# Decoder layer on one core: attention of the last row issued later, the first gate/up tile decoded in the first row's prologue and kept in DRAM, four products of zeros at TensorE's start

## The reference, cut to what matters

```python
x = _layernorm(x + attn(x, weight_qkv, weight_proj))           # causal, over the outer axis of length 4
x = _layernorm(x + ssm(ctx_1024, x, in_proj_w, conv_w, ...))   # state space scan over 512 steps, 16 states
x = _layernorm(x + ffn(x, lut, gate_idx, up_idx, down_idx))

def step(state, xs):                                           # the scan, for each of 4 rows
    d_t, B_t, C_t, u_t = xs
    dA = jnp.exp(d_t[..., None] * A)
    state = state * dA + (d_t * u_t)[..., None] * B_t[:, None, :]
    y_t = jnp.einsum('ben,bn->be', state, C_t)
    return (state, y_t)

def _ghost_linear(x, idx, lut):                                # weights are 4-bit indices into 16 values
    w = lut[idx]
    return jnp.einsum('bsh,oh->bso', x, w)
gate = _ghost_linear(x, gate_idx, lut)
up = _ghost_linear(x, up_idx, lut)
h = jax.nn.silu(gate) * up
return _ghost_linear(h, down_idx, lut)
```

## Time and profile before

| | |
|---|---|
| median of 3 runs | 990.57 us (990.4 to 994.05) |
| the profiled execution's own time | 990.59 us |
| its span in the trace | 988.8 us |
| prologue, until DVE's first scan | 0 to 55.0 us |
| scan of the four rows | 55 to 538 us |
| transition, until the first gate/up product | about 552 to 602.6 us |
| feed-forward | 602.6 to 988.8 us |
| busy share of the span | PE 88%, DVE 77%, ACT 68%, POOL 49% |

### The profile page before, as it was taken

One profiled execution on the slowest core, in us unless ns is written; L12 is line 12 of the kernel. 1 busy time (PEld: TensorE's weight loads), 2 busy tenths in 40 slices (PEclk: granted clock), 3 DMA queues, 4 the chain that ended last, 5 costly groups with the idle time before them and its releaser, 6 DMA issues.

```text
span 988.8 us, 11890 instructions
## 1 busy us (share of the span) xinstructions
PE 869.3 (88%) x3824; PEld 626.4 (63%) x3824; DVE 765.2 (77%) x1066; ACT 672.4 (68%) x994; POOL 481.3 (49%) x445
## 2 busy tenths in 40 slices
PE   6879888787878897787989879899999999899997
PEld 3547654465544674456545457787777778688885
DVE  3797899877998879986788666888888888355442
ACT  4698985789956899668696464777777776242321
POOL 0079867799767998669676631221112111001000
PEclk9789777999779797787979988999999999899998
DMA  8167979589996799967999222111111110223221
GB/s 259 39 168 177 209 161 229 117 221 245 210 224 122 204 241 210 224 125 202 208 289 277 83 96 86 46 61 42 42 42 44 62 42 22 75 86 107 86 64 53
DMA packets 49908, 135.99 MB, mean 138 GB/s; under 512 B 5364, under 2 KB 13684, under 8 KB 41156
## 3 DMA queue, kind: packets, MB, share of 16 engines
q0 software_dynamic: 8064, 58.72, 30.9%
q1 hardware_dynamic: 40432, 76.44, 23.1%
q10 hardware_dynamic: 1364, 0.25, 0.2%
HBM read 57.93 MB, written 78.51 MB: 138 GB/s over the span
## 4 chain that ended last, share of the span: by engine, by line
PE 26%; issue 23%; DVE 23%; ACT 19%; POOL 5%; DMA 4%; DVEq 1%; ACTq 0%; POOLq 0%; SPq 0%
DVE state L1191 6%; PE banks L606 5%; ACT decay L893 5%; PE banks L720 5%; ACT scaled L882 5%; PE banks L744 4%; DVE leaf L1219 3%; DVE w_gu L1219 3%; PE banks L644 3%; PE banks L548 3%; DVE conv_in L1094 3%; POOL state L1442 2%; ACT leaf L1001 2%; DMA hT<-y_scratch 2%; DMA y_scratch<-state 1%
## 5 line engine op out<-in xcount | busy, mean ns | idle before, releaser
L1442 POOL TENSOR_TENSOR state<-state,crep 128x512 f32<-128x512 f32 x243 | 334.8, 1603 | 85.9 <-DVE state L1191 79.7
L1191 DVE TENSOR_TENSOR_SCAN state<-decay,banks 128x512 f32<-128x512 f32 x243 | 280.7, 1202 | 54.2 <-PE banks L644 44.6
L720 PE MATMUL banks<-x2T,wgu 128*128 128x512 f32 x1056 | 246.3, 393 | 4.8 <-DVE hT L1270 4.1
L644 PE MATMUL banks<-ident,scaled 128*128 128x128 f32 x1024 | 175.9, 314 | 69.1 <-DVE state L1191 49.7
L720 PEld LDWEIGHTS banks<-x2T,wgu 128*128 128x128 f32 x1056 | 197.9, 189 | 52.1 <-DVE hT L1270 11.3
L644 PEld LDWEIGHTS banks<-ident,scaled 128*128 128x128 f32 x1024 | 136.2, 161 | 143.1 <-DVE state L1191 63.4
L893 ACT ACTIVATE decay<-delta,negA 128x512 f32<-128x512 f32 x256 | 169.9, 722 | 77.6 <-DVE state L1191 69.8
L882 ACT ACTIVATE scaled<-duT,BT 128x512 f32<-128x512 f32 x256 | 163.8, 720 | 0.0
L1001 ACT ACTIVATE leaf<-idx_sb,table,table_gap 128x1024 f32<-128x1024 uint8 (+1 forms) x132 | 129.4, 1022 | 6.8 <-DVE w_down L1219 3.2
L1219 DVE COPY_PREDICATED leaf<-idx_sb,leaf 128x1024 f32<-128x1024 uint8 (+1 forms) x88 | 94.1, 1069 | 7.1 <-issue 6.1
L1534 POOL TENSOR_TENSOR pool_wait_here<-minus_half 128x1 f32<-128x1 f32 x22 | 4.3, 193 | 180.6 <-DVE w_gu L1219 116.2
(11 more groups left out here) (140 smaller groups left out, 1155.6 us busy)
## 6 DMA issues: line engine op xcount, KB each, us to landing
y_scratch<-state POOLq DMA_DIRECT2D x52, 1024.0 KB, 8.5
crep<-c_scratch SPq DMA_DIRECT2D x64, 256.0 KB, 5.4
idx_sb<-in_idx SPq DMA_DIRECT2D x11, 512.0 KB, 3.5
xT_sb<-in_xT SPq DMA_DIRECT2D x16, 256.0 KB, 4.8
y_scratch<-u SPq DMA_DIRECT2D x4, 1024.0 KB, 6.1
y_scratch<-state SPq DMA_DIRECT2D x4, 1024.0 KB, 6.3
leaf<-x_scratch SPq DMA_DIRECT2D x16, 256.0 KB, 2.8
out<-leaf SPq DMA_DIRECT2D x16, 256.0 KB, 2.0
```

The source lines that it names most:

```text
L644: last = nc.tensor.transpose(banks[:, k % NB, lc * LQ:(lc + 1) * LQ], scaled[:, g % SR, lc, et * P:(et + 1) * P], ident[:])
L720: last = mm(banks[:, 2 * tb + w, :], wgu[par][:, w, ws, t * P:(t + 1) * P], x2T[:, tb, xs, t, :], start=t == 0 and n == 0, stop=t == HT - ...
L1191: V.tensor_tensor_scan(state[:, g % GR, et, :], decay[:, k % DR_RING, :], banks[:, k % NB, :], 0.0, ALU.mult, ALU.add).then_inc(scan_ready, 1)
L1442: G.tensor_tensor(state[:, g % GR, et, :], state[:, g % GR, et, :], crep[:, g % CR, :], ALU.mult)\
```

## The change

Three edits in one, and what they entail.

1. LAST_ATT_AT, LAST_PROJ_AT and LAST_RES_AT: in the last row four attention jobs, two projections and two residuals stand later; ACT's copies of them, its `normalized`, and POOL's `norm_factors` move with them.
2. The gate/up tile 0 is decoded in the prologue, in space that the scan does not use yet (`state` for the leaves, `scaled` for the indices, `decay` for the table): all eight leaves on POOL, seven predicated copies on DVE, the result stored to `w0_scratch` by SP early in the first row and loaded into `w_gu` late in the last row. FIRST's decoding in the transition goes, on ACT, DVE and POOL, and the loads of SECOND and of the first `down` tile are issued where the loads of FIRST and SECOND were, two states later. POOL's second `gate_row` comes behind two of its reciprocal roots.
3. PE runs WARM = 4 products of zeros before it waits for `ip`; POOL fills the zeros.

```diff
+        WARM = 4
-        LAST_ATT_AT = {(3, 0): 3, (3, 1): 0, (4, 0): 2, (5, 0): 1}
+        LAST_ATT_AT = {(3, 3): 3, (4, 0): 0, (4, 2): 2, (6, 1): 1}
-        LAST_PROJ_AT = {(5, 1): 3, (5, 3): 2, (6, 1): 1, (6, 3): 0}
+        LAST_PROJ_AT = {(5, 1): 3, (5, 3): 2, (7, 0): 1, (7, 2): 0}
-                LAST_RES_AT = {(5, 2): 3, (6, 0): 2, (6, 2): 1, (7, 0): 0}
+                LAST_RES_AT = {(5, 2): 3, (6, 0): 2, (7, 1): 1, (7, 3): 0}
...
+        FIRST_MUX = [(0, 1, 1), (2, 3, 1), (0, 2, 2), (4, 5, 1), (6, 7, 1), (4, 6, 2), (0, 4, 3)]
...
@@ SP
                 load_xT(0)
+                sp.dma_start(first_words, idx[0, :, 0:2 * H]).then_inc(first_idx_in, 16)
                 sp.dma_start(wqkv[:], wqkvT.rearrange("(t p) n -> p t n", p=P)).then_inc(wqkv_in, 16)
...
+                        if n == 0 and b == 0:
+                            sp.wait_ge(first_mux_ready, 7)
+                            sp.dma_start(w0_scratch, first_leaf(0)).then_inc(first_stored, 16)
...
-                        if b == S - 1 and n == 11:
+                        if b == S - 1 and n == 13:
                             sp.dma_start(table[:], lut.to_broadcast([P, 16])).then_inc(lut_in, 16)
-                            load_idx(*FIRST)
+                            sp.wait_ge(first_stored, 16)
+                            sp.dma_start(w_gu[:].rearrange("p w n -> p (w n)"), w0_scratch).then_inc(first_in, 16)
                             load_idx(*SECOND)
+                            load_idx("down", 0)
...
@@ PE
+                pe.wait_ge(zeros_ready, 1)
+                for _ in range(WARM):
+                    mm(banks[:, 7, :], state[:, 0, 0, 0:P], state[:, 0, 0, :], start=True, stop=True)
                 pe.wait_ge(ip_in, 16)
...
@@ ACT
+                act.dma_start(first_table, lut.to_broadcast([P, 16])).then_inc(first_lut_in, 16)
                 act.wait_ge(ch_in, 16)
...
                 act.wait_ge(gap_ready, 1)
-                leaves(*FIRST, early)
+                high_part(0, 0)
                 norm_apply(0)
-                leaves(*FIRST, (4, 5))
                 norm_apply(1)
                 x2T_hi(0)
-                leaves(*FIRST, (6,))
...
@@ DVE
+                def first_selects(steps):
+                    for m in steps:
+                        kept, other, bit = FIRST_MUX[m]
+                        dve.wait_ge(first_leaf_ready, max(kept, other) + 1 if m < 6 and bit == 1 else 8)
+                        if m in (2, 5, 6):
+                            dve.wait_ge(first_mux_ready, m)
+                        V.memset(first_wait[:, m:m + 1], 0.0)
+                        V.copy_predicated(first_leaf(kept), first_bit(bit), first_leaf(other)).then_inc(first_mux_ready, 1)
...
+                dve.wait_ge(first_lut_in, 16)
+                first_pairs = first_table.rearrange("p (j two) -> p j two", two=2)
+                V.tensor_tensor(first_gap, first_pairs[:, :, 1], first_pairs[:, :, 0], ALU.subtract).then_inc(first_gap_step, 1)
+                dve.wait_ge(first_gap_step, 1)
+                V.tensor_scalar(first_gap, first_gap, 0.5, None, ALU.mult).then_inc(first_gap_step, 1)
                 dve.wait_ge(ch_in, 16)
                 for et in range(ET):
                     earlier_taps(0, et)
+                    if et == 1:
+                        dve.wait_ge(first_idx_in, 16)
+                        V.tensor_scalar(first_words, first_words, float(SPREAD), None, ALU.mult).then_inc(first_bits_step, 1)
+                    elif et == 2:
+                        dve.wait_ge(first_bits_step, 1)
+                        V.tensor_scalar(first_words, first_words, BYTE_BITS, None, ALU.bitwise_and)\
+                            .then_inc(first_bits_step, 1)
...
+                first_selects(range(5))
                 softplus(0, (0, 1))
                 softplus(0, (2, 3))
+                first_selects((5, 6))
                 head_products(0, 3)
...
-                MUXES = [(FIRST, (0, 1)), (FIRST, (2, 3)), (FIRST, (4, 5)), (FIRST, (6,)), (SECOND, ()),
-                         (SECOND, (0, 1)), (SECOND, (2, 3)), (SECOND, (4,))]
+                MUXES = [(), (), (), (), (), (0, 1), (2, 3), (4,)]
...
@@ POOL
+                G.memset(state[:, 0, 0, :], 0.0).then_inc(zeros_ready, 1)
                 G.memset(minus_half[:], -0.5).then_inc(half_ready, 1)
                 pool.wait_ge(half_ready, 1)
+                pool.wait_ge(first_gap_step, 2)
+                pool.wait_ge(first_bits_step, 2)
+                for j in range(8):
+                    G.tensor_tensor(first_wait[:, 8 + j:9 + j], minus_half[:, 0:1], minus_half[:, 0:1], ALU.add)
+                    G.tensor_scalar(first_leaf(j), first_bit(0), first_gap[:, j:j + 1], first_table[:, 2 * j:2 * j + 1],
+                                    ALU.mult, ALU.add).then_inc(first_leaf_ready, 1)
...
                 gate_row(1)
-                last_leaf(*FIRST)
+                stage2_rstd(0)
+                stage2_rstd(1)
                 gate_row(2)
-                for k in range(5):
+                for k in range(2, 5):
                     stage2_rstd(k)
```

65 lines of the change are left out of this document (39 added, 26 removed).

## The result

| | before | after |
|---|---|---|
| median of 5 runs | 990.57 us (990.33 to 994.05) | 1001.19 us (998.55 to 1001.91) |
| profiled execution, its span | 990.59, 988.8 us | 998.55, 996.7 us |

The changed kernel is slower by 0.88%: the ratio is 1.0088, 95% interval 1.0069 to 1.0106. Measured once more beside the later experiments it was 1.0097 (1.0076 to 1.0118). The two medians stand further apart than the ratio says: 10.6 us, 1.07%. The median lies 7.5 us above the forecast and 1.2 us above the upper end of the range; the ratio on 990.57 us gives 999.3 us, 5.6 us above the forecast and just inside.

What follows compares the result with a forecast made beforehand. The prediction took DVE's work and waits to bound the prologue, PE waits and adding transfers the last row, DVE's low parts the transition. Terms 9.0 + 0.5 - 6.4 = +3.1 us on 990.59 gave 993.7 us, range 985 to 1000.

Steps and rivals of the forecast that it cites:

- rival (c): Whole kernel slower: late table, slow kv products; prologue +12, last row +2, transition -5, 999.6 us; chance 0.27.
- Prologue, +9.0: Up to the first scan: late table, index operations, leaves and copies delay it by 9.0 us, to 64.0 us.
- the point of decision of rival (c): Prologue: a table later than 13.5 us or a leaf chain longer than 15 us would decide for rival (c).
- the zeros' gain: Prologue: products of zeros bring `in_proj`'s first bank 2.0 us earlier, but DVE's wait for the table loses it.
- Last row, +0.5: Last row: `hT` lands 1.75 us earlier, `rest_summed` costs 2.2 us more; sum +0.5 us.
- In the last row no wait of DVE on PE over 3 us: Last row, expected sign: DVE's long waits on PE go, while waits on `y_scratch<-state` grow longer.
- The 2.2 us for `rest_summed` on an idle PE: Row's end: PE's last sums finish some 9 us ahead of `hT`, so `rest_summed` starts slowly, costing 2.2 us.
- Transition, -6.4: Transition: without copies between statistics and shift, residual(4) loses its 4.31 us wait and 2.1 us slow start; -6.4 us.
- a gate/up start less than 5 us closer to `rest_summed`: Transition, sign of a wrong forecast: gate/up start less than 5 us closer to `rest_summed` than before.
- Storing and loading the tile: Store costs nothing; 1.25 MB instead of 1 MB stands ahead of `hT` in SP's queue, +0.75 us.
- Feed-forward: Feed-forward: no edit there, so no change in time was forecast.
- Rival (b): Last row pays: DVE's 11.66 us of waits turn into 6 us at the row's end, 984 us; chance 0.2.

Runs made afterwards that it cites:

- f2: Changed kernel with DVE's two operations on the first table moved from ahead of the taps to behind the second tile's taps; ratio to before 1.0030.
- e3: Changed kernel without the decoding in the prologue, `w_gu` loaded from the raw indices (first tile's weights wrong); 992.43 us, ratio to before 1.0008.
- g1: Changed kernel unaltered, measured again on the chip of g2 to g4; 1001.18 us, ratio to before 1.0097.
- f4: Changed kernel with POOL's gating of row 2 moved back ahead of the first two reciprocal roots; ratio to before 1.0072.
- f1: Changed kernel with ACT's copy of band 1 in the last row one group sooner (n == 5 instead of 6); 993.52 us, ratio to before 1.0001.
- g3: Changed kernel with the edits of f1, f3 (which includes f2) and f4 together; 985.77 us, ratio to before 0.9950.
- g4: g3 with the first tile's words loaded behind `wqkv` and the table's and words' operations behind all taps; 986.20 us, ratio to before 0.9945.
- g2: Kernel before with the last row's later attention alone, but ACT's copy of band 1 at n == 5; 988.85 us, ratio to before 0.9977.
- e2: Kernel before with the last row's later attention alone, copy of band 1 at n == 6; 997.61 us, ratio to before 1.0042.
- e4: Kernel before with PE's four products of zeros alone; ratio to before 0.9997.
- e1: Changed kernel with the last row's attention, projections and residuals back at their old places; 999.58 us, ratio to before 1.0086.
- f3: f2 with the predicated copies spread around the softplus and the third waiting for four leaves instead of eight; ratio to before 1.0037.

## Where the prediction was right, and where wrong

The time was forecast as 993.7 us, most likely within 0.5% of before; it came out 0.88% slower, at the size of rival (c), 999.6 us. That (c) meets it is in part chance: its terms were +12, +2 and -5 us, and +9.76, +3.97 and -4.80 were measured. By the forecast's terms:

**Prologue, +9.0: right, measured +9.76** (up to +11.0 in the traces with the same prologue), step by step. The table was put at 12.0 us and landed at 14.07; by the point of decision of rival (c) (later than 13.5 us) that part of (c) came true. The taps began at 14.39, not 12.4 us. The two operations on the indices took 0.68 us each as taken. The leaves were put at 20.5 to 34.1 us and ran from 22.53 to 35.45, the chain 12.9 us long and not 13.6, with two leaves held by copies, 1.12 and 1.10 us more each, where 1.3 each were added. This is the case that the rows of before didn't show, a leaf held by a copy; "SBUF — State Buffer" of the Trainium skill, section "SBUF: two separate sides", had it, and the trace agrees. The softplus came at 39.12 (38.2), the first scan at 64.75 us (64.0). The later table put the start of the leaves 2.0 us later than forecast; of that 1.35 were left at their end, since the chain was shorter, 0.9 at the softplus and 0.75 at the first scan.

That the zeros' gain is lost behind the table is shown too: with the table's operations moved (f2) the taps begin at 10.44 us. That the prologue's loss isn't hidden is shown by e3, 7.9 us at the end.

**Last row, +0.5: the step that failed; measured +3.97** (first scan to residual(0); +5.03 in g1 and +6.09 in f4, with the same code up to there). The forecast had `hT` land 1.75 us earlier relative to the first scan, and it landed 1.50 later. The prediction followed the moved jobs on PE, where the three waits of 11.66 us do go, and the adding transfers, where the waits do grow, from 3.7 to 7.9 us, but not ACT's copies. The change moved the copy of band 1 from n == 4 to n == 6 while PE's job moved from group 5 to group 6; ACT's list has a group's decays, which wait for scans, ahead of the copy; the projection at (7, 0) waits for the copy, the transposes for DVE's next scans stand behind the projection on PE. A ring through three engines, 6.09 us. "In the last row no wait of DVE on PE over 3 us" was the sign, and it showed wrong. With the copy one group sooner (f1) the distance is 495.65 us, 1.54 less than before, near the forecast's 1.75; in g3 and g4 it is 2.9 and 4.3 less. The 2.2 us for `rest_summed` on an idle PE came true, 2.47, but they too hang on this copy: in f1, g2, g3 and g4 PE's sums end at most 1.8 us ahead of `hT`'s landing and not 7.5, and it takes 3.6 to 3.7 us.

**Transition, -6.4: right in its mechanism, measured -4.80.** The prediction had POOL's second gating end "some 3 us before PE reaches it", and looked only at who waits for its result; but it ran while DVE wanted its shift, and the two excluded each other: 4.46 us for 0.16. The rule on the shared port had been used for copies and leaves and not for this pair. With the gating moved the transition is 39.84 us in f4 and 40.40 in g3, -7.0 and -6.45 against before, and the forecast's -6.4 is met. residual(4) waited 1.22 us (not at all in f4 and g3), residual(7) kept its wait, 3.69 us. One of the signs named for a wrong forecast, a gate/up start less than 5 us closer to `rest_summed`, appeared: 50.39 us before, 48.06 after. It could not tell much, for the forecast's own terms, -6.4 in the transition and +2.2 in `rest_summed`, bring the two only 4.2 us closer.

**Storing and loading the tile**, +0.75 us ahead of `hT`: not seen apart. From issue `hT` took 22.6 us, and 22.12 before.

**Feed-forward**, no change: -1.0 us, and up to -2.5 in g3. The traces place it. From gate/up to the end of PE's last wait in there, 3.49 us long in each (to 858.46 us before, 867.50 after, 853.77 in g3), the three take 255.9 to 256.1 us. In the 15 us behind it the granted clock is 0.81, 0.89 and 1.00, and from the wait's end to the end of the kernel they take 130.34, 129.20 and 127.63 us. My estimate of what the clock costs in these 15 us is 15 x (1 - clock): 2.85, 1.65 and 0 us, which fits the differences. The other traces fall in the same three groups: 0.81 or 0.82 in e2, e4 and g2, 0.89 in g1, e1, e3 and f2 to f4, 1.00 in f1 and g4. So these microseconds are TensorE's clock after one wait; why it differs from kernel to kernel is not shown, nor whether all their executions share it.

The sum of +3.1 missed by 4.8 us on the span: 0.8 from the prologue, 3.5 from the last row, 1.6 from the transition, -1.0 from the feed-forward. The other 2.6 us are that the profiled execution was the fastest of its five. Rival (b), the last row pays, was at the wrong end for this kernel, but what it describes exists: with the copy placed well the attention is worth -0.23% alone (g2).

Open as well is how much of a prologue gain arrives: f2's first scan is 3.7 to 5.0 us sooner than in the five traces with the changed kernel's prologue, its `rest_summed` 1.3 us sooner than in after, 3.0 than in g1 and 3.9 than in f4, while by the ratios 5.7 to 6.6 us arrive.

## What to carry to other kernels

When a job moves in one engine's hand-written list, walk round the whole ring: which engine copies its output away, what stands ahead of that copy in its list, and whether any of it waits for the engine that the job was to relieve. An edit measured alone can have the wrong sign because its partner is one place off (e2 and g2 differ by one number, 0.65%). Where two engines exclude each other on a port, look at every pair that overlaps in time, also at the instruction of two columns: it waits as long as a large one.

## What of the hardware was not expected

- Issuing a transfer of 8 KB took 3.57 us on ACT's queue, behind one of single elements that took 1.31 us to issue, and held ACT's first function load from 4.17 to 7.78 us; it landed 9.9 us after its issue started.
- An operation of DVE on 128x2 elements took 4.46 us beside a gating of 128x2048 on POOL, 4.51 us, and 2.30 us beside POOL's low part, 2.35 us.
- The same 24 kv products took 5.42 us in six of the traces with zeros (e1, e3, e4, f1, g3, g4; waits for `wqkv` of 1.42 to 3.52 us ahead of them) and 7.0 to 7.1 us in the other five (after, g1, f2, f3, f4; waits of 2.76 to 3.30 us). The slow ones ran at a lower clock: in each half of their first 5 us the granted clock is between 0.50 and 0.87, and 1.00 in the six. So a wait of such a length doesn't decide alone whether PE's next products take longer. It moves the softplus: 33.20 us in f3 with 7.11 us, 31.33 us in g3 with 5.42.
